# Rounded split products ahead of layer 0's experts, ranks from prefix sums, and second biases as one stacked product, in a two-layer perceiver kernel

## The reference, cut to what matters

```python
# layer 0's block (an: 512 tokens x 512; 31 experts, 3 chosen, hidden 512)
shared = gelu(an @ sh_w1 + sh_b1) @ sh_w2 + sh_b2
aff = softmax(an @ router_w + router_b); topv, topi = top_k(aff, 3)
gates = sum(one_hot(topi) * topv)                       # 512 x 31
routed = sum_e gates[:, e] * (gelu(an @ re_w1[e] + re_b1[e]) @ re_w2[e]) + gates @ re_b2
out = shared + routed + an + attn_out
# layer 1's cross-attention: keys and values of a context, projected ahead of need
k = ctx @ L1_xattn_Wk ; v = ctx @ L1_xattn_Wv
# layer 1's block: the same shape of work with 16 experts, 2 chosen, SiLU(w1) * w3,
# hidden 704, and gates @ ffn_b2 added
```

## Time and profile before

| | |
|---|---|
| median of 3 runs | 1692.97 us |
| profiled execution, its own time | 1693.26 us |
| its span from first to last instruction | 1691.5 us |
| busy share: PE / VectorE / ScalarE / GpSimd | 98% / 60% / 48% / 14% |
| chain of work that ended last, PE's share | 94% |
| granted TensorE clock, mean | 0.992 |

### The profile page before, as it was taken

How to read it: one execution, slowest core, us unless ns; L and a number is a source line. 1 busy time by engine, 2 the same in 40 slices (tenths; PEclk the granted TensorE clock), 3 DMA queues, 4 the chain that set the end, 5 groups by cost and what they waited for, 6 DMA issues and landing times.

```text
span 1691.5 us, 27328 instructions
## 1 busy us (share of the span) xinstructions
PE 1654.2 (98%) x10623; PEld 1297.2 (77%) x10623; DVE 1017.8 (60%) x2083; ACT 812.6 (48%) x1613; POOL 240.0 (14%) x321
## 2 busy tenths in 40 slices
PE   8999999999999999999999999999999899999997
PEld 6777777777777666555999986777767688799996
DVE  6334344434456886532666575767664856599995
ACT  5333334333434536422655564545545443387884
POOL 0100000000002302431111112311100303021111
PEclk9999999999999999999999999999999999999998
DMA  6011010102042003036999962111231143599994
GB/s 257 26 75 51 26 50 26 50 26 95 6 162 100 1 1 150 4 124 214 377 390 389 384 238 77 50 45 39 82 129 47 68 181 101 212 348 376 373 375 102
DMA packets 44671, 246.54 MB, mean 146 GB/s; under 512 B 5897, under 2 KB 6401, under 8 KB 21744
## 3 DMA queue, kind: packets, MB, share of 16 engines
q1 hardware_dynamic: 32256, 216.63, 33.9%
q0 software_dynamic: 7664, 19.68, 4.1%
q10 hardware_dynamic: 4608, 8.33, 1.3%
HBM read 229.01 MB, written 16.13 MB: 145 GB/s over the span
## 4 chain that ended last, share of the span: by engine, by line
PE 94%; DVE 2%; ACT 2%; issue 1%; POOL 1%; DMA 1%; POOLq 0%; SPq 0%; ACTq 0%; DVEq 0%
PE bank L714 29%; PE bank L281 11%; PE bank L2510 7%; PE bank L287 5%; PE bank L905 3%; PE bank L3589 3%; PE bank L933 3%; PE bank L3069 2%; PE bank L1623 2%; PE bank L844 2%; PE bank L1308 2%; PE bank L2119 2%; PE bank L2121 2%; PE bank L2120 2%; PE bank L1680 2%; PE bank L1596 1%
## 5 line engine op out<-in xcount | busy, mean ns | idle before, releaser
L714 PE MATMUL bank<-split 128*128 128x512 f32 x2160 | 521.2, 395 | 0.0
L714 PEld LDWEIGHTS bank<-split 128*128 128x128 f32 x2160 | 397.7, 188 | 90.2 <-issue 5.3
L281 PE MATMUL bank<-arena,weights 128*128 128x128 f32 (+1 forms) x1024 | 130.0, 285 | 1.8 <-DVE arena L2083 1.8
L281 PEld LDWEIGHTS bank<-arena,weights 128*128 128x128 f32 x1024 | 121.3, 192 | 11.1 <-issue 7.8
L913 ACT COPY normed<-bank 128x512 f32<-128x512 f32 x128 | 68.9, 592 | 121.1 <-PE bank L905 121.1
L876 DVE TENSOR_REDUCE small<-bank 128x1 f32<-128x512 f32 x64 | 43.9, 687 | 132.0 <-PE bank L844 132.0
L774 DVE COPY arena<-bank 128x512 f32<-128x512 f32 x76 | 52.5, 691 | 113.3 <-PE bank L714 113.3
L757 ACT COPY arena<-bank 128x512 f32<-128x512 f32 x76 | 44.6, 588 | 138.3 <-PE bank L714 102.7
L2510 PE MATMUL bank<-up_high_r,tok_r 128*128 128x352 f32 x512 | 108.2, 323 | 0.0
L895 ACT ACTIVATE normed<-bank,small 128x512 f32<-128x512 f32 x64 | 44.1, 690 | 124.0 <-DVE small L878 123.7
L2510 PEld LDWEIGHTS bank<-up_high_r,tok_r 128*128 128x128 f32 x512 | 86.5, 188 | 0.0
(11 more groups left out here) (435 smaller groups left out, 3295.0 us busy)
## 6 DMA issues: line engine op xcount, KB each, us to landing
weights<-in_L_ffn_re_w SPq DMA_DIRECT2D x62, 1024.0 KB, 10.3
weights<-in_L_w SPq DMA_DIRECT2D x20, 1408.0 KB, 8.2
arena<-in_ctxT SPq DMA_DIRECT2D x23, 1024.0 KB, 5.0
arena<-in_L_w SPq DMA_DIRECT2D x12, 1408.0 KB, 9.2
weights<-in_L_w_full SPq DMA_DIRECT2D x10, 1280.0 KB, 9.5
weights<-in_L_ffn_sw SPq DMA_DIRECT2D x9, 1024.0 KB, 4.9
expert_out<-arena ACTq DMA_DIRECT2D x31, 256.0 KB, 8.3
arena<-in_L_w_full SPq DMA_DIRECT2D x6, 1280.0 KB, 11.3
```

The lines of the kernel that those rows point to most:

```text
L281: s = pe.matmul(out, w[:, k, j0:j0 + m], rhs(k), start=(k == 0), stop=(k == KT - 1))
L714: s = pe.matmul(bank[:, :], still, moving, start=(n == 0), stop=(n == len(order) - 1))
```

## The change

1. Keys, values and the shared expert's second product in layer 0 become split products. ScalarE and VectorE get 20 split steps of their own for them, and one for the second biases' rows (`PLAIN_SPLITS`).
2. `route_vector` also makes running sums of the choices over the four token tiles; `rank_tensor` is two matmuls with all tiles side by side, and `count_tensor` is one.
3. The gates are split into high and low parts that stand side by side (high, low, high), the second biases' rows are stacked to match (high, high, low), and `bias_tensor` is one fp32r matmul with both in the contraction.
4. SyncE loads `x1_k` and `x1_v` ahead of the shared weights, the context ahead of `e0_w2`, and `e1_w1`, `e2_w2` and `e1_w2` ahead of `list_sync`.
5. In layer 0's expert loop the rows of expert 1 are turned before expert 0's up product.
6. In layer 1 the turned gates come after tile 4. For the last expert the high parts of w2 get a buffer of their own and the down product a bank of its own, and ScalarE's and VectorE's orders there change.

```diff
@@ layouts @@
+    PLAIN_AT = {"weight_high": 0, "weight_low": 5632, "ctx_high": 8192, "ctx_low": EXPERTS_END, "w2_high": 10240, "hid_low": 3456}
...
@@ selfattn_vector / selfattn_scalar, before the last turned tile @@
+        for k in range(KT):
+            plain_split_vector(dve, ("k", k))
+        for k in range(KT):
+            plain_split_scalar(act, ("k", k))
@@ route_vector @@
             self.wait(dve, "gates", 1)
+            dve.tensor_copy(self.sums[:, 0, :], self.used[:, 0, :])
+            own(dve.tensor_tensor(self.sums[:, 1, :], self.used[:, 0, :], self.used[:, 1, :], ALU.add))
+            own(dve.tensor_tensor(self.sums[:, 2, :], self.sums[:, 1, :], self.used[:, 2, :], ALU.add))
+            dve.tensor_tensor(self.sums[:, 3, :], self.sums[:, 2, :], self.used[:, 3, :], ALU.add).then_inc(self.raised("gates"), 1)
@@ rank_tensor, parts_vector, count_tensor, gates_tensor, bias_tensor @@
+            pe.matmul(rank_bank[:, 0:NT * n], tri[:, :], self.used.rearrange("p i n -> p (i n)"), start=True, stop=False)
+            self.wait(pe, "gates", 2)
+            pe.matmul(rank_bank[:, n:NT * n], ones[:, :], self.sums[:, 0:NT - 1, :].rearrange("p i n -> p (i n)"),
+                      start=False, stop=True).then_inc(self.raised("ranked"), 1)
...
+            dve.tensor_copy(parts_r[:, :, self.last:self.last + n], self.gates)
+            dve.tensor_copy(parts_r[:, :, 0:n], self.gates).then_inc(vec.sem, vec.up())
+            dve.wait_ge(vec.sem, vec.n)
+            dve.tensor_tensor(parts_r[:, :, n:2 * n], self.gates, parts_r[:, :, 0:n], ALU.subtract).then_inc(self.raised("gates"), 1)
...
+            pe.matmul(count_bank[:, 0:n], ones[:, :], self.sums[:, NT - 1, :], start=True, stop=True).then_inc(self.raised("counted"), 1)
...
+        def gates_tensor(self, pe, turn_bank):
+            self.wait(pe, "gates", 3)
             for i in range(NT):
-                for j in range(i + 1):
-                    s = pe.matmul(rank_bank[:, i * n:(i + 1) * n], ones[:, :] if j < i else tri[:, :], used[:, j, :],
-                                  start=(j == 0), stop=(j == i))
...
-            pe.matmul(bank[:, :], self.gatesT[0:self.n, i * P:(i + 1) * P], self.b2[0:self.n, :], start=True, stop=False)
+            pe.matmul(bank[:, :], self.gatesT_r[0:self.rows, i * P:(i + 1) * P], self.b2_r[0:self.rows, :], start=True, stop=False)
@@ down_tensor, layer 1 @@
+        def down_bank(self, ex):
+            return banks[2 if ex == E1 - 1 else 6]
...
-                if m == 0 and ex:
+                if m == 0 and ex == E1 - 1:
+                    self.wait(pe, "silu", E1)
+                elif m == 0 and ex:
                     self.wait(pe, "out_a", ex)
@@ plain_tensor @@
+        for k in range(KT):
+            if g == 0:
+                pe.wait_ge(plain_low, PLAIN_NO["ctx", k])
+            elif g == KT:
+                pe.wait_ge(plain_low, PLAIN_NO["v", k])
+            for a, b in THREE:
...
@@ experts0_sync @@
+        for name, waits in (("x1_k", (self_mm.sem, self_mm.at(9))), ("x1_v", (self_mm.sem, self_mm.at(10))), ("sh_w1", (self_mm.sem, self_mm.at(17))),
...
         sp.wait_ge(out_mm, 3 * NT)
         x1.load_context(sp, 0)
+        load_weight(sp, "e0_w2")
+        load_weight(sp, "e1_w1")
...
-        sp.dma_start(moe0.b2[0:E0, :], A["L0_ffn_re_b2"]).then_inc(b2_in, 16)
+        sp.dma_start(moe0.b2[0:moe0.rows, :], A["L0_b2_rows"]).then_inc(b2_in, 16)
+        moe0.wait(sp, "routed", 1)
+        load_weight(sp, "e2_w2")
+        sp.wait_ge(sh_mm.sem, sh_mm.at(KT))
+        load_weight(sp, "e1_w2")
         moe0.list_sync(sp)
+        sp.wait_ge(sh_mm.sem, sh_mm.at(2 * KT))
+        load_weight(sp, "e2_w1")
@@ experts0_tensor @@
-        for m in SH_ORDER[2:]:
-            project_into(pe, banks[m][:, :], w1.view, m * P, P, lambda k: xnT[:, k, :]).then_inc(sh_mm.sem, 1)
+        m = SH_ORDER[2]
+        project_into(pe, banks[m][:, :], w1.view, m * P, P, lambda k: xnT[:, k, :]).then_inc(sh_mm.sem, 1)
+        half_tile(SH_ORDER[3], 0)
         moe0.rank_tensor(pe, banks[4])
+        half_tile(SH_ORDER[3], 1).then_inc(sh_mm.sem, 1)
...
             if m == 0:
-                moe0.count_tensor(pe, banks[5], banks[6])
+                moe0.count_tensor(pe, banks[5])
+            if m == 2:
+                moe0.gates_tensor(pe, banks[6])
+        pe.wait_ge(plain_low, PLAIN_NO["b2", 0])
         for i in range(NT):
...
+            if i == 0:
+                pe.wait_ge(plain_low, PLAIN_NO["hid", SH_ORDER[-1]])
+            for n, (k, (a, b)) in enumerate((k, z) for k in range(KT) for z in THREE):
...
         moe0.turn_rows(pe, 0)
-        pe.wait_ge(x1.kv_a.sem, x1.kv_a.at(2 * KT))
+        pe.wait_ge(x1.kv_a.sem, x1.kv_a.at(KT + 2))
+        moe0.turn_rows(pe, 1)
...
-            if ex + 1 < E0:
+            if ex and ex + 1 < E0:
                 moe0.turn_rows(pe, ex + 1)
@@ experts0_vector @@
         moe0.route_vector(dve, row("router_b"), banks[4])
+        for k in range(KT):
+            plain_split_vector(dve, ("ctx", k))
         moe0.place_vector(dve, banks[4], banks[5])
+        moe0.parts_vector(dve)
+        for s in [("w2", k) for k in range(KT)] + [("b2", 0)] + [("hid", m) for m in SH_ORDER] + [("v", k) for k in range(KT)]:
+            plain_split_vector(dve, s)
@@ experts1_scalar, the last expert @@
-                moe1.w2_scalar(act, ex, w2, (0, 1))
-                moe1.hidden_scalar(act, ex)
-                moe1.w2_scalar(act, ex, w2, (2,))
+                moe1.w2_scalar(act, ex, w2)
+                moe1.hidden_scalar(act, ex, (0,))
                 moe1.out_scalar(act, ex - 1)
+                moe1.hidden_scalar(act, ex, (1,))
```

More of the change, by code:

```diff
@@ L1899, in __init__ @@
             self.gates = L(NT, n)
+            if layer == 0:
+                L(NT)
+                parts = Layout(GATE_PARTS_AT[0])
+            else:
+                assert S.at <= GATE_PARTS_AT[1]
+                parts = Layout(GATE_PARTS_AT[1], small, 1024)
+            assert L.at == GATES_AT[layer]
             self.gatesT, self.b2 = L(TOK), L(DIM)
+            self.rows, self.last = GATE_ROWS[layer], GATE_LAST[layer]
+            self.gate_parts, self.gate_parts_r = parts(NT, self.rows), blocks(gate_parts_r[layer][:, :], NT)
+            self.gatesT_r, self.b2_r = gatesT_r[layer], bias_r[layer]
             self.list_buffers(L)
             self.gather = [arena[:, ARENA - (i + 1) * DIM:ARENA - i * DIM] for i in range(4)]
-            self.totals = {"routed": 1, "shifted": 1, "exped": 1, "gates": 1, "ranked": 1, "slots": 2 - layer, "counted": 1,
+            self.totals = {"routed": 1, "shifted": 1, "exped": 1, "gates": 3, "ranked": 1, "slots": 2 - layer, "counted": 1,
                            "over": 1, "turned": 1, "gatesT": 1,
@@ new lines, in bias_rows_scalar, with bias_rows_vector, count_tensor @@
+        def bias_rows_scalar(self, act):
+            act.wait_ge(b2_in, self.b2_value)
+            return act.copy(self.b2_r[0:self.rows, :], self.b2[0:self.rows, :])
+        def bias_rows_vector(self, dve):
+            low = self.b2_r[self.last:self.rows, :]
+            return dve.tensor_tensor(low, self.b2[self.last:self.rows, :], low, ALU.subtract)
+        def count_tensor(self, pe, count_bank):
+            n = self.n
+            pe.matmul(count_bank[:, 0:n], ones[:, :], self.sums[:, NT - 1, :], start=True, stop=True).then_inc(self.raised("counted"), 1)
@@ L2549, in turned_part, with hidden_scalar @@
             return banks[(1, 7)[z]][:, 0:b - a], slice(a, b)
-        def hidden_scalar(self, act, ex):
-            for z in range(2):
+        def hidden_scalar(self, act, ex, parts=range(2)):
+            for z in parts:
                 bank, c = self.turned_part(z)
@@ L2671, in plain_tensor, with plain_split_vector @@
+    def plain_split_vector(dve, s):
+        dve.wait_ge(plain_high, PLAIN_NO[s])
+        if s[0] == "b2":
+            moe0.bias_rows_vector(dve).then_inc(plain_low, 1)
+            return
+        high, low, src = plain_split_tensors(s)
+        dve.tensor_tensor(low, src, high, ALU.subtract).then_inc(plain_low, 1)
     def plain_tensor(pe, g):
         m, bank = g % KT, banks[g % KT]
-        if g < KT:
-            project_into(pe, bank[:, :], weights["x1_k"].view, m * P, P, lambda k: x1.ctxT[:, k, :]).then_inc(x1.kv_mm.sem, 1)
-        else:
-            project_tokens(pe, bank[:, :], lambda k: x1.ctxT[:, k, m * P:(m + 1) * P], weights["x1_v"].view, 0,
-                           DIM).then_inc(x1.kv_mm.sem, 1)
+        for k in range(KT):
[4 more added lines that the diff above has]
+            for a, b in THREE:
+                if g < KT:
+                    still, moving = plain_weight[a][:, k, m * P:(m + 1) * P], plain_ctx[b][:, k, :]
+                else:
+                    still, moving = plain_ctx[a][:, k, m * P:(m + 1) * P], plain_weight[b][:, k, :]
+                s = pe.matmul(bank[:, :], still, moving, start=(k == 0 and a == b == 0), stop=(k == KT - 1 and a == 1))
```

(14 more changed lines are left out.)

163 lines of the change are left out of this document (108 added, 55 removed).

## The result

The changed kernel takes 1671.01 us (median of 4 runs, 1670.13 to 1672.37), the kernel before 1692.78 (4 runs, 1691.47 to 1693.23): a ratio of 0.9875, 95% interval 0.9862 to 0.9887. The forecast was 1672.4 us. The profiled execution took 1672.37 us, its span is 1670.6, and the mean granted clock 0.994.

What follows compares the result with a forecast made beforehand. TensorE's own work was taken as the bound, 94% of the chain. Layer 0 10.8, layer 1 7.7 and tail 2.0 make 20.5 us: 1693.26 - 20.5 - 0.29 = 1672.4 us, 8-in-10 range 1667.5 to 1678.5.

Steps and rivals of the forecast that it cites:

- Layer 0's products and ranks, 12.2 + 2.3: Layer 0: rounded keys, values, shared output and biases win 12.2 us; fewer rank and count instructions win 2.3 us.
- The splits, 0.3: Layer 0: TensorE waits 0.3 us for VectorE's split steps, whose chain ends at 749.1.
- splits are the bound: Rival, chance 0.04: VectorE's subtracts in layer 0 take half as long again under GpSimd's traffic; about 1678 us.
- The list, 4.0 + 0.7: Layer 0's value tiles: TensorE waits 4.0 us for the scattered list, then loses 0.7 us to slow matmuls.
- the list comes in time: Rival, chance 0.22: scatters aren't stretched or land sooner, wait 0 to 1.5 us, no slow clock; 1667.7 to 1669.4 us.
- First experts, 1.3: Layer 0's first experts: two pauses for copies of turned rows become one, a turn moves into it; 1.3 us won.
- Layer 1's ranks and clock, 2.3 + 1.4: Layer 1: fewer rank and count instructions win 2.3 us, no slow clock behind them wins 1.4 us.
- Layer 1's biases, 4.0: Layer 1: a tile with its bias falls from 3.99 to 2.99 us; four tiles win 4.0 us.
- Tail, 2.0: Kernel's end: TensorE need not wait for the fifteenth output, the last add starts earlier; 2.0 us, bounds 0 and 3.5.
- Experts starting 12 to 13 us earlier: Sign given beforehand: the expert work after layer 0's block would start 12 to 13 us earlier than before.
- A granted clock of 0.50 inside layer 0's block would make the forecast wrong: Sign against the forecast: TensorE at the 1.2 GHz level anywhere in layer 0's block would refute it.
- slower: Rival, chance 0.02: clock at 0.50 for layer 0's whole block between 737 and 774, costing 29.6 us; 1702 us.

Runs made afterwards that it cites:

- e4: Changed kernel with layer 0's keys and values again as float32 products, splits kept; median 1.8 to 2.8 us over the changed kernel's two.
- e11: The changed kernel itself once more, nothing edited, on one chip with its partner run; 1671.16 to 1673.35 us, ratio 0.9881 to the kernel before.
- e7: Changed kernel with expert 1's rows turned after expert 0's up product again; expert 0's down product starts 3.18 us later against its up product; no median given.
- e5: Changed kernel with layer 1's ranks and counts in the old form (10 and 4 narrow products); f-g 4.10 us longer, profiled execution 1679.79 us.
- e2: Changed kernel with layer 1's gate and bias products over 96 rows (further ones zero) instead of 48; median 1670.67 us.
- e8: Changed kernel without TensorE's branch to the part for layer 0 experts with more than 128 tokens; median 1673.38 us.
- e1: Changed kernel with layer 0's list load waited for one value tile later; median 1672.46 us.
- e9: Changed kernel with the list waited for one value tile later and 96-row gate and bias products in layer 1; median 1670.42 us.
- e12: Changed kernel with later list wait and layer 1's 96-row products, repeated on one chip beside the unedited one; 1668.55 to 1670.81 us, ratio 0.9865 to the kernel before.
- e3: Changed kernel with layer 0's subtracts for second weights, hidden rows and values cut to 8 columns; scatters 14.14 us, list wait 2.27 us; no median given.
- e10: Changed kernel with GpSimd's three adds of layer 0's last token tile cut to 8 columns; VectorE's four subtracts 2.50 us; no median given.

## Why the prediction was right, point by point

The forecast was 20.5 us in the profile, and the spans differ by 20.9 (the medians by 21.8). By the stages: a-b 9.9 (62.59 - 52.67), b-c 1.55, f-g 6.6, the tail 2.3, and 0.5 already there at mark a. That last 0.5 can't be credited to the change: mark a lies anywhere from 724.12 to 725.71 in the thirteen profiles of the changed forms, and at 725.22 before.

- *Layer 0's products and ranks, 12.2 + 2.3.* The periods are as forecast: 0.23 us a product, 2.97 a tile with biases, ranks 0.42. Less the list's cost and the branch below, 14.5 - 3.7 - 0.7 = 10.1 is left, and 9.9 was measured. Of these only keys and values have an experiment of their own (e4); shared output, layer 0's biases and ranks, and the moved loads rest on the timelines.
- *The splits, 0.3.* TensorE never waited for one. The chance given to "splits are the bound" had more behind it than the text saw: the key weights' subtracts took twice their price, and only 0.19 us of cover was left. I had priced them by a row with no adds of GpSimd's beside it.
- *The list, 4.0 + 0.7.* This was the term in which the case was decided, and it came out as 2.2 + 1.5 = 3.7. Its parts were off in both directions: the stretch 1.0 us instead of 2.1, the list's load 2.6 to land instead of 2.0, the landing of the scatters 6.4 instead of 7.7, the slow clock twice what I gave it. In nine profiles with this order the wait was 0.69 to 3.27 us. So the rival "the list comes in time" is another execution of the same kernel as much as another theory: e11's profile, with 1.00 us and no slow clock, is that rival's case.
- *First experts, 1.3.* 1.55 by the trace and by e7.
- *Layer 1's ranks and clock, 2.3 + 1.4.* Measured 4.0 (f-g's 6.6 less the biases' 2.6), and 4.1 by e5, which also shows that the narrow products bring the clock down.
- *Layer 1's biases, 4.0.* This is the term that missed by most: "13 rounded matmuls take 2.99" prices a 48-row product as a 128-row one. It measured 2.6, as the tile takes 3.34, and e2 gives the missing 1.5 back.
- *Tail, 2.0.* 2.1 at the last add, by the mechanism given, 2.3 to 2.7 at the end of the span.
- *Not forecast:* 0.66 us at the branch ahead of expert 0's rows (e8).

So the biases' miss (1.4 less) and the branch (0.7 less) were met by the list's lower cost (1.0 more), the splits' 0.3, layer 1's ranks (0.3), first experts and tail (0.5), and the 0.5 us that lie ahead of mark a.

The mechanism was right: the terms are where they were said to be, and the list became the wait. That the total came within half a microsecond of the profiled pair's difference is luck. Misses of opposite sign cancelled, and between profiles the list's wait differs by 2.6 us, c-d by 3.4 and e-f by 2.2; in the profiled pair c-d and e-f happened to be equal.

Two of the signs given beforehand did not come as stated. "Experts starting 12 to 13 us earlier" was 10.4 (787.81 to 777.39), and does not follow from the sum, which has 12.2 + 2.3 - 0.3 - 4.0 - 0.7 = 9.5 up to there. "A granted clock of 0.50 inside layer 0's block would make the forecast wrong": it was 0.50 for some 3 us behind the list's wait, the very thing that the sum priced at 0.7 and that cost 1.5. As a sign it was drawn too wide: the drop over the whole block, of the rival "slower", did not come.

Open: why the landing of twelve scatters spreads over 2 us; what the idle time inside expert 1's up product is (1.27, 1.21 and 0.99 us in e1, e9 and e12, 0.66 in e3, 0.17 in e10). It stands at the same instruction each time and at no semaphore, so code that comes late is a candidate. The Trainium skill, "Runtime: NRT & Kernel Launch", section "Instruction fetch mechanics", has the sequencer fetch its next page while the current one runs; a fetch held up by other transfers would fit. The traces don't bear it out, though. In e1 a packet of the instruction queue starts at 778.6 to 778.8, right ahead of the restart at 779.09, but by its own recorded time of 0.97 us it ends behind that restart, and in e12 no instruction packet starts between 777.4 and 781.3, with the restart at 778.57. No run separates the causes.

## What to carry to other kernels

When TensorE's work ahead of a long chain of other engines and DMAs shrinks, price that chain first: here rounding keys and values won 5.4 us of products and kept about 2 (e4), because a list that had been in time now ended the wait. Move the consumer behind more work, but look at what stands behind it as well. Price an operation by a row of its own shape, rows of the contraction included, and an engine's step by a row with the same neighbours at work.

## What the runs showed of the hardware that I had not expected

- **A granted clock that falls in steps and not in every execution.** c-d holds the same products in all fourteen profiles and takes 12.89 us in three, 14.58 in nine and 16.25 in two; e-f takes 36.6 in eight and 34.45 in six. In e-f the clock is low behind the 2.68 us wait in all fourteen. In the eight it falls twice more, some 9 and 30 us later (windows of 3 us there read 0.56 to 0.87); in the six those windows read 1.00. The window from 1258 to 1262, inside c-d, of the changed kernel, then of e1, then of e9:

```profile
1258.00:1262.00 4.00, 3.81 (x16) 1.00 0.23 98
```

```profile
1258.00:1262.00 4.00, 4.00 (x7) 0.63 0.00 0
```

```profile
1258.00:1262.00 4.00, 4.00 (x11) 0.50 0.10 43
```

  Clocks of 1.00, 0.63 and 0.50 for the same work, behind the same small idle times (0.73 and 0.45). Such a step is as large as most terms of this change, so an edit worth 1 to 2 us is seen in its stage and not in the median.
- **Slow clock behind a wait.** Ahead of the value tiles, waits of 2.18 us and more (2.27, 3.23, 3.27) were followed by 0.50 to 0.61 for three microseconds or more; waits of 2.09, 1.62, 1.00, 0.79 and 0.69 were followed by 1.00. The two nearest are too close to each other for the wait's length alone to be the cause.
- **A 48-row rounded product costs more than a 96-row one.** It adds 0.37 us to a tile (3.34 against 2.97), with the same 512 columns: its own weight load and the next one are not covered by the matmul ahead (e2). Rows of zeros that fill it up to 96 win that back.
- **A branch shows behind short products.** 0.66 to 1.54 us of idle behind rounded products, none behind float32 ones (e4), none without the branch (e8).
